# A selective scan on one core: the skip term by transposes of a scaled x, and a fifth buffer of states

## The reference, cut to what matters

```python
def step(hst, ins):
    dt_t, B_t, C_t, x_t = ins
    dA = jnp.exp(dt_t[:, :, None] * A)
    hst = hst * dA + (dt_t * x_t)[:, :, None] * B_t[:, None, :]
    y_t = jnp.einsum('bds,bs->bd', hst, C_t)
    return (hst, y_t)
...
y = jnp.swapaxes(ys, 0, 1) + xs * Dskip
return y * jax.nn.silu(z) @ out_w
```

## Time and profile before

| what | value |
|---|---|
| median of 3 runs | 3308.7 us (3304.81 to 3312.47) |
| the profiled execution's own time | 3316.36 us |
| its span | 3314.5 us |
| mean granted TensorE clock | 0.970 |
| busy share: PE, DVE, ACT, POOL | 92%, 87%, 88%, 88% |
| first scan, last scan start | 194.5 us, 3268.7 us |

### The profile page before, as it was taken

How to read it: one execution, slowest core, us unless ns; L and a number is a source line. 1 busy time by engine, 2 the same in 40 slices (tenths; PEclk the granted TensorE clock), 3 DMA queues, 4 the chain that set the end, 5 groups by cost and what they waited for, 6 DMA issues and landing times.

```text
span 3314.5 us, 71769 instructions
## 1 busy us (share of the span) xinstructions
PE 3058.3 (92%) x23032; PEld 2760.6 (83%) x23032; DVE 2884.0 (87%) x3203; ACT 2904.8 (88%) x6357; POOL 2911.3 (88%) x1552
## 2 busy tenths in 40 slices
PE   8778999999999999999999999999999999998877
PEld 6568988898888988889888898888888898887766
DVE  2269999899989998899998999899988999989985
ACT  1189999898989989899998999899898989989993
POOL 0069999998999999999998999999999999999995
PEclk6699999999999999999999999999999999999998
DMA  5011111111111111111111111112111111111210
GB/s 179 0 42 45 45 46 54 43 52 44 46 51 45 52 44 47 51 50 44 46 54 44 51 45 45 53 45 52 44 47 50 51 46 45 45 50 44 55 47 26
DMA packets 163039, 162.61 MB, mean 49 GB/s; under 512 B 17610, under 2 KB 156874, under 8 KB 162644
## 3 DMA queue, kind: packets, MB, share of 16 engines
q1 hardware_dynamic: 162644, 157.69, 17.5%
HBM read 154.44 MB, written 3.18 MB: 48 GB/s over the span
## 4 chain that ended last, share of the span: by engine, by line
PE 50%; ACT 23%; issue 11%; DVE 8%; POOL 7%; DVEq 0%; ACTq 0%; POOLq 0%; DMA 0%; SPq 0%
PE ps L1263 13%; ACT dA L584 12%; PE ps L1247 12%; ACT uBT L570 6%; PE ps L1010 6%; POOL hst L417 5%; DVE hst L909 5%; PE ps L1245 4%; PE ps L1082 3%; PE ps L1019 3%; PE ps L1057 3%; PE ps L1066 1%; PE ps L1255 1%; PE ps L1131 1%; POOL uBT L430 1%
## 5 line engine op out<-in xcount | busy, mean ns | idle before, releaser
L417 POOL TENSOR_TENSOR hst<-hst,C_sb 128x1024 f32<-128x1024 f32 x1024 | 2447.3, 2407 | 176.1 <-DVE hst L909 172.7
L909 DVE TENSOR_TENSOR_SCAN hst<-dA,ps 128x512 f32<-128x512 f32 x2048 | 2376.7, 1203 | 146.3 <-PE ps L1263 112.9
L584 ACT ACTIVATE dA<-dt,A 128x255 f32<-128x255 f32 x4096 | 1745.0, 501 | 1.4 <-DVE hst L909 1.2
L1263 PE MATMUL ps<-ident,hst 128*128 128x128 f32 x8192 | 1240.7, 274 | 46.8 <-POOL hst L417 46.7
L1247 PE MATMUL ps<-ident,uBT 128*128 128x128 f32 x7104 | 1084.5, 275 | 52.6 <-DVE hst L909 39.8
L570 ACT ACTIVATE uBT<-uT,BT 128x512 f32<-128x512 f32 x1376 | 936.4, 717 | 117.3 <-PE ps L1247 89.2
L1263 PEld LDWEIGHTS ps<-ident,hst 128*128 128x128 f32 x8192 | 963.2, 141 | 62.9 <-POOL hst L417 62.2
L1247 PEld LDWEIGHTS ps<-ident,uBT 128*128 128x128 f32 x7104 | 844.6, 142 | 195.3 <-DVE hst L909 69.4
L430 POOL TENSOR_TENSOR uBT<-uT,BT 128x512 f32<-128x512 f32 x400 | 427.2, 1068 | 1.4 <-PE ps L1245 1.4
L1245 PE MATMUL ps<-uBT,uT 128*128 128x128 f32 x2176 | 302.7, 284 | 33.9 <-DVE hst L909 27.9
L1245 PEld LDWEIGHTS ps<-uBT,uT 128*128 128x128 f32 x2176 | 272.9, 197 | 45.7 <-DVE hst L909 35.9
(11 more groups left out here) (146 smaller groups left out, 2176.0 us busy)
## 6 DMA issues: line engine op xcount, KB each, us to landing
C_sb<-c_dram SPq DMA_DIRECT2D x1024, 128.0 KB, 2.9
gate_l<-gate_rows_dram SPq DMA_DIRECT2D x16, 256.0 KB, 3.8
x_att<-in_x_dram SPq DMA_DIRECT2D x8, 256.0 KB, 3.6
w<-in_L_cond_W_dram SPq DMA_DIRECT2D x2, 1024.0 KB
out_dram<-x_glu SPq DMA_DIRECT2D x8, 256.0 KB, 3.1
wg<-in_L_cond_mlp_w_dram SPq DMA_DIRECT2D x3, 512.0 KB, 11.0
w_xp<-_L_cond_fwd_xproj_w_dram SPq DMA_DIRECT2D x1, 1280.0 KB, 12.5
w_xp<-_L_cond_bwd_xproj_w_dram SPq DMA_DIRECT2D x1, 1280.0 KB, 14.4
```

The costliest lines, as they stand in the source:

```text
L417: pool.tensor_tensor(h, h, C_sb[:, n % FED:n % FED + 1, :].to_broadcast([P, KI, NB]), ALU.mult).then_inc(hC_ready.sem, 1)
L584: done = act.activation(dA[:, n % NT, c, lo:hi], dt[:, d, c, lo:hi], ACT.Exp, scale=A[:, d, c, n:n + 1])
L909: dve.tensor_tensor_scan(pair(hst[:, n % NR]), pair(dA[:, n % NT]), ps[:, BANK_U + (2 * n + e) % (2 * NU), :][:, way], 0.0, ALU.mult, ALU. ...
L1263: last = pe.matmul(ps[:, BANK_Y + j, c * P:(c + 1) * P], hst[:, n % NR, c, j * P:(j + 1) * P], ident[:, :], start=False, stop=(n == NS - 1 ...
```

## The change

x is scaled by D in place in `xsT`, on DVE in step 23 of `dts` (one 128x1024 instruction with a broadcast column as second input), and `start_y` becomes eight accumulating transposes against `ident`. `skip_diag` and its eight instructions go. The room (4 KB a partition) holds a fifth buffer of states: `NR` = 5. Since 64 is not a multiple of 5, a pass uses buffers 0 to 3 for its last four states; states 0 to 3 of the next pass follow on those, state 4 takes buffer 4, last used nine states before, and from state 5 on the distance is five. `BEHIND` stays 3.

```diff
-    NR = 4
+    NR = 5
+    reuse = lambda n: NR if n >= NR else NS % NR + (NR if n >= NS % NR else 0)
...
-        skip_diag = sb("skip_diag", [P, 2, KI, P])
...
-                for d in range(2):
-                    for c in range(KI):
-                        dve.tensor_scalar(skip_diag[:, d, c, :], ident[:, :], D_col[:, d, c:c + 1], None, ALU.mult).then_inc(skip_ready, 1)
...
+                    if i == 23:
+                        dve.tensor_tensor(xsT[:, :, :], xsT[:, :, :], D_col[:, d, :].unsqueeze(2).to_broadcast([P, KI, NB]),
+                                          ALU.mult).then_inc(skip_ready.sem, 1)
...
-                    dve.wait_ge(y_mm.sem, y_mm.at(r, e + 1 - 2 * NR))
+                    dve.wait_ge(y_mm.sem, y_mm.at(r, e + 1 - 2 * reuse(n)))
...
-            def start_y(p, d):
+            def start_y(p):
 
+                pe.wait_ge(skip_ready.sem, skip_ready.at(p, 1))
                 pe.wait_ge(g_ready.sem, g_ready.at(p, 0))
                 for j in range(TT):
                     for c in range(KI):
-                        pe.matmul(ps[:, BANK_Y + j, c * P:(c + 1) * P], xsT[:, c, j * P:(j + 1) * P], skip_diag[:, d, c, :],
-                                  start=(c == 0), stop=False, skip_group_check=True)
+                        pe.matmul(ps[:, BANK_Y + j, c * P:(c + 1) * P], xsT[:, c, j * P:(j + 1) * P], ident[:, :],
+                                  start=(c == 0), stop=False, is_transpose=True, skip_group_check=True)
...
-            pe.wait_ge(skip_ready, 2 * KI)
```

More of the change, by code:

```diff
@@ L253, in cond_transformer_mamba_kernel @@
         dve_setup, rows_ready, mods_ready, bn_turns = map(sem, ("dve_setup", "rows_ready", "mods_ready", "bn_turns"))
-        att_mm, att_mods, wqk_ready, skip_ready = map(sem, ("att_mm", "att_mods", "wqk_ready", "skip_ready"))
+        att_mm, att_mods, wqk_ready = map(sem, ("att_mm", "att_mods", "wqk_ready"))
         offset_turns, hT_turns = sem("offset_turns"), sem("hT_turns")
@@ L286, in cond_transformer_mamba_kernel @@
         soft_step, dt_ready, u_ready, g_ready = flow("soft_step", 2), flow("dt_ready"), flow("u_ready"), flow("g_ready", 1, 1)
+        skip_ready = flow("skip_ready")
         uT_mm, uT_ready = flow("uT_mm"), flow("uT_ready")
@@ L1274, in state @@
                     if n == BEHIND and e == 0:
-                        start_y(p, d)
+                        start_y(p)
                     if n >= BEHIND:
```

## The result

The changed kernel takes 3330.4 us in the median of 4 runs (3327.7 to 3336.3), the kernel before 3308.0 us in 4 runs (3304.8 to 3312.5): ratio 1.007, 95% interval 1.0058 to 1.0082, 22.4 us more. I had forecast 3302 us and a range up to 3317; the time lies outside, on the other side. The profiled execution of after took 3332.15 us with a span of 3330.3 us, 15.8 us more than the span of before; the granted clock is 0.968 in the mean, 0.970 before.

What follows compares the result with a forecast made beforehand. No engine bounds throughout: PE and DVE lead by turns, POOL fills the last pass. Terms -14.3 - 3.9 + 12.8 - 1.6 = -7.0 us, from 3308.7 to about 3302 us; range 3288 to 3317.

Steps and rivals of the forecast that it cites:

- Part 1: `start_y` by transposes on PE at the turns between passes: 1.02 us less at each of 14 turns, -14.3 us.
- part 4: Prologue: the eight `skip_diag` instructions go from DVE's chain, -1.6 us.
- Part 2: Fifth buffer: scans start 0.44 us earlier; worth 0 before the softplus, 0.3 us before residuals in 13 passes, -3.9 us.
- the 198 waits: DVE's scans waiting for PE's sums, 112.9 us in all; not 0.44 us gained at each, since PE leads there.
- Part 3: Scaling of x on DVE in step 23: backward +10.2, first forward +1.5, last block's forward +1.1, together +12.8 us.
- The backward term: Scaling in seven backward passes: 1.83 us on DVE, of which about 1.45 reach PE each time, +10.2 us.
- A: Rival: scaling at step 23, both directions, costs more than `start_y` gives; slower, 3318 us; chance 0.14.
- A's threshold: A decides once the scaling's mean cost per pass is above 1.6 us, set against 19.8 us from the other parts.
- D: Rival: PE's slow-clock stretches behind the six loop jumps grow, 1.5 us lost each time; 3311 us; chance 0.06.

Runs made afterwards that it cites:

- nosc4: The changed kernel without the scaling of x (factor D left out) and with four buffers: 3293.3 us, ratio 0.9961 to the kernel before.
- nr4: The changed kernel with four buffers of states instead of five, scaling and transposes kept: 3312.4 us, ratio 1.0021 to the kernel before.
- late4: nr4 with the scaling in the six inner forward passes moved in front of the scan of state 31: 3313.5 us, ratio 1.0017 to the kernel before.
- act4b: The changed kernel with four buffers and the scaling on ACT instead of DVE, a repeat run: 3296.8 us, ratio 0.9961 to the kernel before.
- nosc5: The changed kernel without the scaling of x (factor D left out), five buffers kept: 3311.6 us, ratio 1.0006 to the kernel before.
- act5: The changed kernel with the scaling on ACT instead of DVE, five buffers and new waits kept: 3313.0 us, ratio 1.0009 to the kernel before.
- sel5: nosc5 with the old wait (sum four states before) in states 44 to 55 of backward passes: 3297.9 us, ratio 0.9971 to the kernel before.
- aftersel: The whole changed kernel with the old wait in states 44 to 55 of backward passes: 3307.9 us, ratio 0.9998 to the kernel before.
- act5sel: act5 with the old wait in states 44 to 55 of backward passes: 3301.4 us, ratio 0.9977 to the kernel before.

## Why the prediction was wrong, step by step

**Part 1 and part 4, -14.3 - 1.6 = -15.9 us: right.** nosc4 shows about -13 us of the two together, `start_y` took 0.91 us, DVE's wait at the turn 1.43 us (forecast 1.3). The lower bound, 0 at a turn, fell.

**Part 2, -3.9 us: the step that failed first.** It reads "the head start of 0.44 us is used up in that wait, worth 0". The first half is true: the wait grew from 0.47 to 1.11 us. The value is not 0 but +2.39 us in each of seven passes, 16.7 us. Against it stand the 0.65 us gained in states 8 to 48 of these passes, 4.5 us, so the columns explain 12 us; the pairs of runs give 15 to 16 us for the buffer, and where the other 3 to 4 us are stays open. I treated a wait as a cushion that swallows whatever comes early. But POOL is tied to the scans and not to ACT, so it took the head start along, and the instruction behind the cushion excludes POOL. I had the price formula, 1.08 us plus what is left of POOL's instruction, and had even written its range, 1.1 to 3.4 us; I used it for the new instruction only, never for the four old ones (L832, L835, L839, L843) whose phase the buffer shifts. The trace of before would have given warning: L832 starts at 1319.59, POOL's long L417 at 1320.00, 0.41 us later, so the forecast shift of 0.44 us alone brings POOL's instruction just ahead of the softplus, by 0.03 us. This wasn't one of my rivals: A put the mishap at step 23.

The other claim of part 2, that the 198 waits are no 198 gains since PE leads there, held. But they didn't shrink to 0.08 us as I wrote; 83.8 us in 163 places is 0.51 us each, with another releaser: a head start is gained once, then DVE waits for the force as it had for the sum. What it gave is 0.65 us in the backward states 8 to 48 (from nr4 to after; forecast 0.3) and nothing in the forward columns.

**Part 3, +12.8 us: right in the instruction, wrong in the cover.** The lengths came as written, 1.20 us forward, 1.94 (forecast 1.91) backward, but for the 3.45 us of the one for the last pass, whose share in the total no run separates. The text puts the forward one behind both scans at 1049.36; it stands between them, and the time it gives, 1050.48, is that place. The runs give 0.60 to 0.64%, 20 us. The step that failed is the forward one, "1.5 us of cover for 1.1 us. Cost 0": it cost 1.13 to 1.25 us in six passes, 7 us, since I had read the cover on DVE and not on ACT, which waited for DVE's copies and had none. late4 (0.46 us left) and act4b (0.03) confirm it from two sides, by position and by engine. The backward term, 1.45 us each, can be neither confirmed nor refuted by size: the last column differs by 0.5 us between nr4 and nosc4, by 1.8 between after and nosc5, by 1.1 between nr4 and act4b, and its looseness is as large.

**Rivals.** A had the sign (3318 us) and the smaller half of the cause: between -7.0 forecast and +22.4 measured lie 29 us, of which the scaling has 7 (20 for 12.8), the buffer 20 (16 for -3.9) and the transposes and prologue 3 (-13 for -15.9). A's threshold of 1.6 us a pass doesn't follow from its numbers: 19.8 us over 14 passes are 1.4. D, the clock: as written it did not come, since nr4, with the same scaling and the same real matmuls gone, has a mean granted clock of 0.973 over its ten runs, as before has (0.973 over 24). But the three kernels with the long softplus have 0.968 (after in 4 runs, nosc5 and act5 in 12 each). Six stretches of 3.4 us at half clock, in about 3300 us, are 0.003 of these 0.005, and states 48 to 56 take no longer with them than without; whether the rest of the lower clock costs part of the 3 to 4 us above is not shown.

## What to carry to other kernels

Where two engines exclude each other, an instruction's length depends on the moment at which it comes; an edit that only lifts a wait shifts all such moments, so price the old instructions behind it again, not the new ones alone. Read the cover for an added instruction on every engine that waits for what stands behind it, not only on the engine that runs it. And before an operation goes on an engine of an exclusive pair, look for one outside it: here the same scaling cost 20 us on DVE and 0 to 3 us on ACT, though ACT was as busy.

## What the runs showed of the hardware that was not expected

- The same DVE instruction on the same data took 1.52 to 1.54 us or 3.28 to 3.38 us, by whether it came 0.16 us (0.17 in nr4) into a short instruction of POOL or 0.1 to 0.2 us into one of 2.4 us.
- Four DVE instructions of 0.32 us with one tensor input and a scalar per partition took 4.08 us beside POOL, one over all 1024 elements with two tensor inputs took 1.20: splitting made it worse.
- A standstill of PE of 3.0 to 3.2 us came with 3.4 or 6.8 us at half clock, from about its end on, in 18 of 21 backward passes (six of seven in after, nosc5 and act5), and the scans of states 48 to 56 were no later for it.
- Putting one wait back in 12 states of each backward pass made three kernels faster, by 0.35% (nosc5 to sel5) and 0.72% (after to aftersel), and in act5 to act5sel by 0.32%.
